# Layer 1 of a two-layer graph network selects twelve edge columns of a block on TensorE instead of eleven

## The reference, cut to what matters

```python
def layer0(feat, efeat, W_e, b_e, bias, src, dst):
    ew = (efeat @ W_e + b_e).reshape(E, in_f, out_f)
    msg = jnp.einsum('ei,eio->eo', feat[src], ew)
    summed = jax.ops.segment_sum(msg, dst, num_segments=N)
    cnt = jax.ops.segment_sum(jnp.ones((E,), feat.dtype), dst, num_segments=N)
    return summed / jnp.maximum(cnt, 1.0)[:, None] + bias

def layer1(features, edge_src, edge_dst, edge_type, edge_emb, w_ih, w_hh, b_ih, b_hh):
    A = edge_emb[edge_type].reshape(-1, 16, 16)
    msg = jnp.einsum('emh,eh->em', A, features[edge_src])
    m = jax.ops.segment_sum(msg, edge_dst, num_segments=n_nodes)
    ...  # a GRU cell of m and features gives h_new
    return h_new

x = _layernorm(x + layer0(x, edge_attr_16, ..., src, dst), axis=-1)
x = _layernorm(x + layer1(x, src, dst, edge_type_8, ...), axis=-1)
```

## Time and profile before

| | |
|---|---|
| median of 3 runs | 5712.77 us (5708.83 to 5714.77) |
| the profiled execution | 5721.4 us, its span 5719.6 us |
| TensorE busy (PE) | 5142.5 us, 90% of the span |
| weight loads (PEld) | 4642.5 us |
| VectorE (DVE) | 4200.5 us, 73% |
| ScalarE (ACT) | 3887.2 us, 68% |
| GpSimd (POOL) | 3397.9 us, 59% |

### The profile page before, as it was taken

One profiled execution on the slowest core, in us unless ns is written; L12 is line 12 of the kernel. 1 busy time (PEld: TensorE's weight loads), 2 busy tenths in 40 slices (PEclk: granted clock), 3 DMA queues, 4 the chain that ended last, 5 costly groups with the idle time before them and its releaser, 6 DMA issues.

```text
span 5719.6 us, 131035 instructions
## 1 busy us (share of the span) xinstructions
PE 5142.5 (90%) x41758; PEld 4642.5 (81%) x41759; DVE 4200.5 (73%) x5387; ACT 3887.2 (68%) x5533; POOL 3397.9 (59%) x3559
## 2 busy tenths in 40 slices
PE   6999999999999999999878888888888888888887
PEld 5888888888888888888768888787888878788886
DVE  7888888888888888888856666666666666666666
ACT  6667677767777667766566666666666666667664
POOL 6555556556556556555556666666666656666664
PEclk9999999999999999999989999999999999999998
DMA  3111111111111111111111111111111111111110
GB/s 67 30 33 32 33 31 32 32 32 33 31 31 33 32 33 31 33 31 32 27 20 24 24 24 24 24 22 24 24 24 24 24 24 23 25 22 24 24 23 14
DMA packets 330970, 161.25 MB, mean 28 GB/s; under 512 B 193244, under 2 KB 330011, under 8 KB 330771
## 3 DMA queue, kind: packets, MB, share of 16 engines
q1 hardware_dynamic: 218224, 130.59, 9.2%
q0 software_dynamic: 112512, 29.03, 5.7%
q10 hardware_dynamic: 160, 0.80, 0.1%
HBM read 157.44 MB, written 2.66 MB: 28 GB/s over the span
## 4 chain that ended last, share of the span: by engine, by line
PE 77%; issue 12%; DVE 8%; DVEq 2%; another core or an unknown queue 1%; ACT 0%; POOL 0%; DMA 0%; ACTq 0%; SPq 0%
PE psN L752 59%; PE psM L789 15%; DVE cand L953 3%; DVE z L991 2%; PE psM L770 1%; PE psM L760 1%; DVE z L959 1%; DVEq L997 1%; DVE nodeT L935 1%; PE psM L771 0%; DVEq L934 0%; PE psM L773 0%; PE psM L761 0%; PE psN L893 0%
## 5 line engine op out<-in xcount | busy, mean ns | idle before, releaser
L752 PE MATMUL psN<-table_hi,pick 128*128 128x320 f32 (+1 forms) x13670 | 4047.3, 314 | 159.9 <-issue 107.5
L752 PE MATMUL psN<-table_lo,pick 128*128 128x320 f32 (+1 forms) x13670 | 3965.8, 306 | 9.4 <-issue 9.0
L752 PEld LDWEIGHTS psN<-table_hi,pick 128*128 128x128 f32 x13670 | 2579.1, 189 | 282.4 <-issue 222.5
L578 ACT ACTIVATE pick<-dist 128x640 fp32r<-128x640 bf16 (+1 forms) x2485 | 1788.0, 782 | 1263.0 <-PE psN L752 670.2
L752 PEld LDWEIGHTS psN<-table_lo,pick 128*128 128x128 f32 x13670 | 2580.9, 189 | 11.9 <-issue 10.8
L500 POOL DMA_INDIRECT z<-in_x,idx x1761 | 1685.8, 957 | 1131.4 <-PE psN L752 441.6
L500 POOL DMA_INDIRECT z<-h_rows,idx x1755 | 1685.7, 961 | 1116.4 <-issue 421.3
L570 ACT ACTIVATE dist<-src_mod,neg_node 128x640 bf16<-128x640 uint16 (+1 forms) x2485 | 1968.6, 868 | 4.6 <-DMA src_mod<-src_mod_rows 4.6
L953 DVE TENSOR_TENSOR cand<-psN,grp_hot 128x640 f32<-128x640 f32 (+1 forms) x1492 | 1123.7, 765 | 960.6 <-PE psN L752 630.4
L991 DVE TENSOR_TENSOR z<-psD,z 128x2048 f32<-128x2048 f32 (+1 forms) x750 | 1367.6, 1823 | 55.3 <-issue 31.4
L789 PE MATMUL psM<-z,onehot 128*32 128x273 f32 (+1 forms) x12500 | 845.3, 339 | 321.0 <-issue 266.7
(11 more groups left out here) (108 smaller groups left out, 771.5 us busy)
## 6 DMA issues: line engine op xcount, KB each, us to landing
src_mod<-src_mod_rows SPq DMA_DIRECT2D x249, 192.0 KB
src_mod<-src_mod_rows SPq DMA_DIRECT2D x248, 160.0 KB
z<-in_x,idx POOLq DMA_INDIRECT x1761
z<-h_rows,idx POOLq DMA_INDIRECT x1755
eab<-in_edge_attr SPq DMA_DIRECT2D x125, 200.0 KB
idx<-in_src SPq DMA_DIRECT2D x250, 12.5 KB
dstb<-in_dst SPq DMA_DIRECT2D x250, 14.0 KB
grp<-src_grp SPq DMA_DIRECT2D x249, 5.5 KB
```

The costliest lines, as they stand in the source:

```text
L578: act.activation(pick[j][:, CHUNKS[i], 0:hi - lo], dist[i][:, 0:hi - lo], ACT.Relu, bias=1.0, scale=-1.0).then_inc(l["pick_act"], 1)
L752: mm = pe.matmul(rows[:, :, 0:cells.shape[2]], pick[j][:, c, at:at + P], cells, start=(i == 0 and part == 0), stop=(i == TC - 1 and part = ...
```

## The change

Layer 1 picks 12 columns and gathers 13; layer 0 keeps 11 and 14, with column 19 picked in place of column 20. Layer 1's halves are t0 to t5 and t6 to t11. Its gates become: n0 to n3 and n5 wait for t7 to t10 and t11 of the block before, n6 for its own t0, n7 for the sums, n8, n9 and n11 for their own t2, t3 and t4. The per-block index arrays have 12 entries a partition instead of 11 (`HM`), and the first half's `pick` tile holds six columns. The space of GpSimd's DMA descriptors is set to 8,192 bytes a partition.

```diff
-PICKED = [4, 5, 6, 7, 13, 14, 21, 22, 23, 24, 20]
-H = ((11, 11), (11, 11))
+PICKED = [4, 5, 6, 7, 13, 14, 21, 22, 23, 24, 19, 20]
+H = ((11, 11), (12, 12))
...
-HCUT = [[(0, 5, h) for h in hs] for hs in H]
+HCUT = [[(0, n, h) for h in hs] for n, hs in zip((5, 6), H)]
...
-HALF_1 = 5
+HALF_1 = 6
...
-FIRST_PAIRS = [(5, 6), (6, 8), (8, 10)] + ([(10, 11)] if H[1][0] == 11 else [])
+FIRST_PAIRS = [(6, 8), (8, 10), (10, 12)]
...
-SUMMED = [(0, 4), (4, 6), (6, 10), (10, 11)]
+SUMMED = [(0, 4), (4, 6), (6, 10), (10, 12)]
...
-AFTER_OWN = ([{4: 0, 5: 1, 6: 2, 7: 3, 8: 4, 11: 5, 12: 6}] * 2, [{5: 0, 6: 1, 9: 3, 10: 4, 12: 5}] * 2)
+AFTER_OWN = ([{4: 0, 5: 1, 6: 2, 7: 3, 8: 4, 11: 5, 12: 6}] * 2, [{6: 0, 8: 2, 9: 3, 11: 4}] * 2)
 AFTER_SUMS = (10, 7)
-AFTER_LAST = ([{0: 7, 1: 8, 2: 9, 3: 10}] * 2, [{0: 7, 1: 8, 2: 9, 4: 10}] * 2)
+AFTER_LAST = ([{0: 7, 1: 8, 2: 9, 3: 10}] * 2, [{0: 7, 1: 8, 2: 9, 3: 10, 5: 11}] * 2)
...
-                    g0, g1 = next(g for g in SUMMED if g[0] <= t0 < g[1])
+                    g0, g1 = next((g[0], min(g[1], H[k][buf])) for g in SUMMED if g[0] <= t0 < g[1])
...
-    nc = bacc.Bacc("TRN2", target_bir_lowering=False, num_devices=1)
+    nc = bacc.Bacc("TRN2", target_bir_lowering=False, num_devices=1, dynamic_dma_scratch_size=8192)
```

## The result

The changed kernel takes 6148.99 us (median of 4 runs, 6147.47 to 6161.68) against 5712.85. The ratio is 1.0767, 95% interval 1.0753 to 1.0781: slower by 436 us. The forecast of 6130 us and its range hold. On another chip it took 6154.01 against 5716.01, ratio 1.0764 (1.0746 to 1.0782).

What follows compares the result with a forecast made beforehand. TensorE, nearly full in layer 1 at 22.2 us a block, was taken as the bound. The profiled 5721.4 us plus 417 for layer 1 and 1 for preparation gave 6139, less 8.6 above the median: 6130 us, range 5,560 to 6,260.

Steps and rivals of the forecast that it cites:

- The half of six: ScalarE, layer 1: two `pick` before `sumT` wait for t5, not t4, and grow from 730 to 832 ns, delaying R.
- The size of the hold: Six unbroken gathers: t5 seen 2.25 us after the last starts, Z + 8.9 (Z: t3's start); R 4.7 us later than now.
- R to the sums: TensorE, layer 1: R's 0.49 us and eight picks of 1.46, 11.68 in all; sums start at Z + 22.84.
- The sums: TensorE before t3: 1.72 us alone, 2.77 with one gather beside them, 3.82 with two; one was taken.
- The total: Layer 1: a block of 25.6 us against 22.2, +417 us over 123 blocks; with preparation +1, forecast 6130 us.
- The twelfth pick: TensorE, layer 1: eight picks after R in place of seven, each 1.46 us.
- Descriptor space: GpSimd's gathers: no wait for space, zero; as a bound only, up to 1 us more for each of 13 gathers.
- the gather less: GpSimd, layer 1: 1.26 us a block less on an engine busy 59% of its time; nothing by itself.
- ScalarE's longer instructions: Six-column half: 0.10 us more in each of five `pick` and five `dist`, about 1 us a block; hidden.
- VectorE: Layer 1, double select and longer reduce: +0.66 us a block, covered; bound 81 us; as rival bound 5,795 us, chance 0.05.
- The signs named: Profile after: R idle 4 to 5 us, gathers at 1.26 us, `pick` idle about 5, PE digits 7, waits 1.00 and 0.63 gone.
- The rival of signals in time: Layer 1: t5 seen at Z + 4.8, R at Z + 6.57; faster, 5,626 us with one gather in the sums; chance 0.31.

Runs made afterwards that it cites:

- Experiment 2: Kernel before with halves of six and five picks and the smaller descriptor space: 5028.55 us, ratio 1.0228, without late signals; 5976.26 us, ratio 1.0434, with them.
- experiment 3: Changed kernel with `sumT` copied ahead of the first two `pick`: against the kernel before, 5095.05 us, ratio 1.0364, without late signals; 5797.04 us, ratio 1.0133, with them.
- experiment 4: Changed kernel with halves of five and seven: against the kernel before, 5098.03 us, ratio 1.0368, without late signals; 5765.38 us, ratio 1.0067, with them.
- experiment 6: Changed kernel with n12's old gate on its own t5 put back, a run of five gathers: 6084.98 us, 69 less than the changed kernel on this chip.
- experiment 7: Changed kernel with R put behind t6 and t7 in TensorE's order: 5852.61 us, ratio 1.0236 to the kernel before.
- experiment 8: Kernel before with two gates moved, n10 to t5 and n12 to t7: 5913.18 us, ratio 1.0322.
- experiment 1: Kernel before with only the descriptor space set to 8,192 bytes a partition: 4915.83 us, ratio 0.9999, on a chip without late signals.
- experiment 9: Changed kernel with `sumT` copied first and n10 gated on t5, n12 on t7: 5601.29 us, ratio 0.9781 to the kernel before.

## Why the prediction was right

- **The half of six: right, and the cause.** The `pick` instructions wait for t5, `sumT` stands behind them, R behind it. Experiment 2 gets 249 of the 436 us from this edit alone, experiment 3 gets 357 of 438 back by the queue order alone, experiment 4 gets all but 38 back by waiting for t4. These overlap and don't add up: with the half of six, the gates and the twelfth pick cost more than the 38 they cost without it.
- **The size of the hold: too long.** t5 was put at Z + 8.9; it was seen at Z + 8.2 in the block shown and at 7.9 on the average of 89. The step that failed is "2.25 after the start of the last gather": it was read from blocks in which TensorE still worked when the last gather started, and holds in those (experiments 3, 6, 7, 8). Where it had stopped before, as in the changed kernel, the signal came some 1 us earlier on the average, and as forecast in only a part of the blocks. R came at Z + 9.6 on the average, not 10.67. The prediction named this at its end, as what could go wrong; it went wrong by 1.0 us and not by more.
- **R to the sums: too short.** Forecast 12.17 us; in the block shown 4048.12 - 4034.37 = 13.75, on the average 14.2. The missing terms are the wait for outer part 2 with 0.4, and the lower clock after the stall with the rest, 1.6 to 1.7 us a block, in line with the 1.6 of the block shown.
- **The sums: too long.** One gather beside them was taken at 1.05 us. They take 1.7 us: n5 and n6, gated later, start in front of them in nearly all blocks. One is still running when the sums begin in 0.7 of the blocks, as the one at 4047.43, and costs next to nothing: those sums took 1.72.
- **The total.** -1.0 for R, +2.1 behind it, -1.1 for the sums: 25.6 us a block was forecast and 25.6 measured. The mechanism was right; that the time agrees to 0.3% is luck, three errors cancelling. The first R and the last one show where the span's 426 us arose, before and in the changed kernel:

```profile
2921.24 0.49 PE L773 MATMUL psM<-sumT,A 128*128 128x128 f32 x2 [0.35 <-issue]
...
5671.71 0.49 PE L773 MATMUL psM<-sumT,A 128*128 128x128 f32 x2 [0.35 <-ACT sumT L557]
```

```profile
2939.07 0.49 PE L773 MATMUL psM<-sumT,A 128*128 128x128 f32 x2 [1.76 <-issue]
...
6097.89 0.49 PE L773 MATMUL psM<-sumT,A 128*128 128x128 f32 x2 [0.35 <-ACT sumT L557]
```

  From R to R it is 2750.5 us before and 3158.8 after: layer 1 grew by 408 us, where 417 were forecast. The other 18 us lie ahead of it, where the prediction had +1 for the preparation and nothing for layer 0. The first pick starts 1.4 us later, at 31.8 us for 30.4, as forecast for the preparation; most of the rest, some 15 us, arises in layer 0.
- **The twelfth pick** costs 1.46 us a block where TensorE is full (experiments 3 and 4), as reckoned. With late signals the sums that the new gates shorten by 2.2 us a block make up for it (experiment 4); what it costs there by itself was not measured.
- **Descriptor space, the gather less, ScalarE's longer instructions:** nothing, as costed. The first is shown by experiment 1, but only for the chip without late signals. With them it is open: on one chip the first R comes at 2930.11 in experiment 8, with the old space, and at 2945.64 in the second run of experiment 2, with the new one and the same layer 0. That is 15 us, near the 18 above, from one execution each. For the others only the engines' idle time speaks.
- **VectorE** was held to be covered. In the changed kernel it is but for 0.4 us; with the stall gone (experiment 3, late signals) it is the bound, by t5 seen 1.4 us later than before and by the 0.7 us that its chain is longer.
- **The signs named** came: R's idle, six gathers at 1.26 us, ScalarE's wait (4.9 and 6.8 us in two blocks). The wait of 1.00 is gone; of the 0.63 there are 0.4 left on the average. The digits are 8, not 7: a TensorE at the lower clock counts as busy.
- **The rival of signals in time:** there is a chip on which the signals do come in time. The kernel before takes 4915 us there; the changed kernel was not run on it. Experiment 2 shows `pick` started on t5 at Z + 4.73 on that chip, some 0.03 us after t5's end. The increment tail of the Trainium skill, "TensorE: Matmul & The Clock Gate", section "The cost: per-tile semaphore tail", agrees with that chip, where t4 and t5 are seen at once, and not with the others, where t5 is seen 2.9 us late in the kernel before.

## What to carry to other kernels

An engine that waits for a buffer delays all that stands behind it in its queue: put the copy that another engine needs ahead of the wait, or let the wait be for something finished long before. Look at when a released engine starts, not only at when its releaser ended: on some chips an unbroken run of indirect gathers keeps TensorE's signals back until it ends. The copy put ahead brought the same twelve picks from 7.6% slower to 1.3% slower; gates that cut the runs as well, with none left long elsewhere, brought them to 2.2% faster. And count a stall of TensorE of 3 to 4 us as more: some half of its length is paid again at the lower clock.

## What the runs showed of the hardware

- **Chips differ.** The same program took 4915 us on one chip and 5713 to 5727 on three occasions on others. On the slower ones signals of TensorE are late during runs of gathers (t5 by 2.9 us), and the sums have gaps of 0.34 to 0.47 us when gathers start beside them; on the faster one neither shows. The gathers themselves are alike, 0.96 us each 1.26. Why chips differ stays open; a verdict on such a kernel holds for its kind of chip. The kernel of experiment 9 was not run on the fast kind; there I would expect its twelfth pick to cost there what it costs in experiments 3 and 4.
- **The hold ends some 2.2 us after the run's last gather starts, often earlier if TensorE has stopped.** Seen after the start of the run's last gather: 2.25 us (before), 2.1 (experiment 6), 2.4 (3 and 8), 2.15 (7), but 1.2 to 1.3 on the average where TensorE had stopped before it. In ordinary blocks t4, three gathers into the run, passes, and t5, four in, doesn't; in the uncommon block of the earlier trace rows t4 was late too. What holds them was not found.
- **The clock.** After 3.85 us idle TensorE was granted 0.98 for 1.2 us, then 0.50 for 3.2 us. Over layer 1 from 3,200 to 5,400 us the granted clock was 0.92 in the changed kernel (3.5 us in front of R a block) and 0.89 in experiment 8 (2.5 us in front of the sums). With a wait of 1.4 us in front of R, in experiment 7, it was 0.97, and in experiment 9 it was 1.00.
